# Expert tiles: half of each weight piece's subtractions a turn later, and one list multiply on another engine

## The reference, cut to what matters

```python
x = x + tanh(g_xattn) * attention(layernorm(x), ctx, ctx, fside, W1, b1, W2, b2)
h = layernorm(x).reshape(-1, 256)
route = softmax(h @ router_w + router_b, axis=1)
max_prob, max_ind = route.max(1, keepdims=True), argmax(route, 1)
for e in range(8):
    a, g = split(h @ w1[e], 2, axis=1)          # w1[e]: 256 x 2048
    y = silu(a) * g @ w2[e]                     # w2[e]: 1024 x 256
    out = where((max_ind == e)[:, None], y, out)
x = x + tanh(g_ffn) * out * max_prob
```

## Time and profile before

| | us |
|---|---|
| median of three runs | 448.81 |
| the profiled execution, its own time | 449.49 |
| its span, first to last instruction | 447.7 |
| TensorE (PE) busy | 401.3 |
| GpSimd (POOL) busy | 243.7 |
| VectorE (DVE) busy | 217.0 |
| ScalarE (ACT) busy | 176.5 |
| the 84 subtractions of L493, busy | 107.1 |
| TensorE's mean granted clock | 0.954 of full |

### The profile page before, as it was taken

How to read it: one execution, slowest core, us unless ns; L and a number is a source line. 1 busy time by engine, 2 the same in 40 slices (tenths; PEclk the granted TensorE clock), 3 DMA queues, 4 the chain that set the end, 5 groups by cost and what they waited for, 6 DMA issues and landing times.

```text
span 447.7 us, 9834 instructions
## 1 busy us (share of the span) xinstructions
PE 401.3 (90%) x2431; PEld 346.5 (77%) x2432; DVE 217.0 (48%) x527; ACT 176.5 (39%) x338; POOL 243.7 (54%) x324
## 2 busy tenths in 40 slices
PE   5998984149989999999999999999999999999990
PEld 4787872027878888888888888888888888888880
DVE  4689899933454443444433444433444434444340
ACT  1167650024443454545532344445433543233230
POOL 2356997221865577887772258728852676232221
PEclk9999897559999999999999999999999999999996
DMA  7950233863333044333442003433331011000010
GB/s 204 360 199 2 95 107 131 85 175 108 118 118 117 23 166 163 135 117 116 134 155 83 27 17 117 134 112 124 117 117 35 4 35 35 24 24 27 24 33 12
DMA packets 29850, 44.01 MB, mean 98 GB/s; under 512 B 8377, under 2 KB 25581, under 8 KB 27791
## 3 DMA queue, kind: packets, MB, share of 16 engines
q1 hardware_dynamic: 24095, 34.45, 24.6%
q0 software_dynamic: 3456, 9.11, 6.3%
q10 hardware_dynamic: 2288, 0.33, 0.5%
HBM read 35.44 MB, written 8.83 MB: 99 GB/s over the span
## 4 chain that ended last, share of the span: by engine, by line
PE 80%; DVE 7%; POOL 6%; DMA 2%; issue 2%; ACT 1%; DVEq 0%; SPq 0%; POOLq 0%; ACTq 0%
PE py L1117 22%; PE pa L1099 21%; PE pg L1099 21%; PE ph L1109 7%; POOL w_lo L415 2%; PE px L1084 2%; DVE x_all L742 1%; PE ps_s L1024 1%; POOL rstd L399 1%; DMA ctx_in<-in_ctx 1%; DVE bn L750 1%; DMA x_sorted<-residual_rows,idx_gather 1%; PE ps_p L968 1%; PE ps_xt L940 1%; DVE x_norm L878 1%
## 5 line engine op out<-in xcount | busy, mean ns | idle before, releaser
L895 DVE TENSOR_TENSOR ht_lo<-ph,ht_hi 128x512 fp32r<-128x512 f32 x70 | 48.4, 691 | 135.4 <-ACT ht_hi L624 135.4
L493 POOL TENSOR_TENSOR w_lo<-staging,w_hi x84 | 107.1, 1304 | 7.3 <-ACT w_hi L645 4.0
L624 ACT CAST ht_hi<-ph 128x512 fp32r<-128x512 f32 x70 | 41.1, 586 | 118.6 <-PE ph L1109 83.4
L1117 PE MATMUL py<-w_hi,ht_hi 128*128 x280 | 81.3, 291 | 0.8 <-DVE out_tile L903 0.8
L1117 PE MATMUL py<-w_lo,ht_hi 128*128 x280 | 78.4, 280 | 0.0
L1117 PE MATMUL py<-w_hi,ht_lo 128*128 x280 | 78.3, 280 | 0.0
L482 POOL DMA_INDIRECT out<-out_tile,idx_now x34 | 34.6, 1019 | 72.6 <-DVE out_tile L903 72.0
L1099 PE MATMUL pa<-w_hi,xt_hi 128*128 (+1 forms) x140 | 58.7, 420 | 0.8 <-ACT xt_hi L606 0.8
L443 POOL DMA_INDIRECT x_sorted<-residual_rows,idx_now x34 | 35.6, 1048 | 39.5 <-DVE x_norm L878 21.4
L1099 PE MATMUL pg<-w_lo,xt_hi 128*128 (+1 forms) x140 | 55.9, 400 | 0.0
L1099 PE MATMUL pg<-w_hi,xt_hi 128*128 (+1 forms) x140 | 55.9, 399 | 0.0
(11 more groups left out here) (168 smaller groups left out, 583.2 us busy)
## 6 DMA issues: line engine op xcount, KB each, us to landing
staging<-in_L_ffn_w SPq DMA_DIRECT2D x24, 1024.0 KB
residual_rows<-x_all SPq DMA_DIRECT2D x8, 516.0 KB, 4.0
x_all<-in_x SPq DMA_DIRECT2D x8, 512.0 KB, 10.1
x_sorted<-residual_rows,idx_now POOLq DMA_INDIRECT x34
out<-out_tile,idx_now POOLq DMA_INDIRECT x34, 2.5
w_in<-in_L_xattn_W SPq DMA_DIRECT2D x2, 256.0 KB, 4.7
ctx_in<-in_ctx SPq DMA_DIRECT2D x1, 308.0 KB
mask_in<-in_fside_1xSxS ACTq DMA_DIRECT2D x1, 308.0 KB, 11.7
```

The costliest lines, as they stand in the source:

```text
L493: lo = nc.gpsimd.tensor_tensor(out=w_lo[:, bass.ds(dst + q * QW, QW)], in0=staging[:, bass.ds(src + q * QW, QW)], in1=w_hi[:, bass.ds(dst ...
L624: nc.scalar.copy(ht_hi[:, j], ph[j][:]).then_inc(hhi_ready[j], 1)
L895: nc.vector.tensor_tensor(out=ht_lo[:, j], in0=ph[j][:], in1=ht_hi[:, j].bitcast(FP32), op=ALU.subtract).then_inc(hlo_ready[j], 1)
L1117: last = mm(py[:, 0:D], ht[:, j, c * P:(c + 1) * P], w[:, bass.ds(slot + (DC * PW + (j * HC + c) * D), D)], start=j == 0 and n == 0, stop= ...
```

## The change

The multiply of round 0 moves from GpSimd to VectorE, between the comparison of round 0 and those of round 1, and the semaphore `token_ready` goes. `low_part` is split into two halves of two subtractions. The first stays where it was, behind the store of the turn. The second comes in the following turn, between the gather and the store, and adds to `w_ready`. Each half reads the piece's number and branches for itself. A last second half stands behind the loop.

```diff
-            end_group = ROUNDS[0][1]
-            pool.wait_ge(col_ready, 1)
-            nc.gpsimd.tensor_tensor(out=col_hot[:, 0:end_group], in0=col_hot[:, 0:end_group],
-                                    in1=token_of[:, 0:end_group].unsqueeze(2).to_broadcast([P, end_group, COLS, B]),
-                                    op=ALU.mult).then_inc(token_ready, 1)
-
...
-            def low_part(t):
+            def low_half(t, half):
 
                 piece = pool.value_load(tile_piece[:, bass.ds(t, 1)], min_val=0, max_val=E * PIECES - 1)
                 with pool.If(piece > 0):
                     src = pool.snap((piece % PIECES) * PW)
                     dst = pool.snap(((piece // PIECES) & 1) * EW + src)
-                    pool.wait_ge(w_hi_ready, piece + (N_CHUNK - PIECES + 1))
-                    for q in range(QUARTERS):
+                    if half == 0:
+                        pool.wait_ge(w_hi_ready, piece + (N_CHUNK - PIECES + 1))
+                    for q in range(half * QUARTERS // 2, (half + 1) * QUARTERS // 2):
                         lo = nc.gpsimd.tensor_tensor(out=w_lo[:, bass.ds(dst + q * QW, QW)],
                                                      in0=staging[:, bass.ds(src + q * QW, QW)],
                                                      in1=w_hi[:, bass.ds(dst + q * QW, QW)].bitcast(FP32),
                                                      op=ALU.subtract)
-                    lo.then_inc(w_ready, 1)
-
+                    if half == 1:
+                        lo.then_inc(w_ready, 1)
 
             def tile(t):
                 index_copies(t)
                 pool.wait_ge(xnorm_ready, t + 2)
                 pool.wait_ge(res_ready, t + 2)
                 gather_rows(t + 2, idx_now[:, 0:1])
+                low_half(t - 1, 1)
                 scatter(t - 1, out_tile)
-                low_part(t)
-
-            low_part(0)
+                low_half(t, 0)
+
+            low_half(0, 0)
             tile(1)
             with pool.Fori(2, total) as t:
                 tile(t)
+            low_half(last_tile, 1)
...
-                slots = nc.vector.tensor_tensor(out=slot_hot[:, at], in0=of_group(slot_iota, P),
-                                                in1=of_token(pos_f[:, 1], P), op=ALU.is_equal)
-                if r == 0:
-                    slots.then_inc(hot_ready, 1)
-                else:
-                    dve.wait_ge(col_ready, r + 1)
-                    nc.vector.tensor_tensor(out=col_hot[:, at], in0=col_hot[:, at], in1=of_token(token_v[:], COLS),
-                                            op=ALU.mult).then_inc(hot_ready, 1)
+                nc.vector.tensor_tensor(out=slot_hot[:, at], in0=of_group(slot_iota, P), in1=of_token(pos_f[:, 1], P),
+                                        op=ALU.is_equal)
+                dve.wait_ge(col_ready, r + 1)
+                nc.vector.tensor_tensor(out=col_hot[:, at], in0=col_hot[:, at], in1=of_token(token_v[:], COLS),
+                                        op=ALU.mult).then_inc(hot_ready, 1)
...
-                if r == 0:
-                    pe.wait_ge(token_ready, 1)
                 pe.wait_ge(hot_ready, r + 1)
```

More of the change, by code:

```diff
@@ L275, in flamingo_block @@
         col_ready = sem("col_ready")
-        token_ready = sem("token_ready")
         hot_ready = sem("hot_ready")
```

## The result

| | before | after |
|---|---|---|
| median, us | 448.29 (447.25 to 449.14, 4 runs) | 456.4 (454.87 to 457.59, 4 runs) |
| the profiled execution, us | 449.49 | 456.28 |
| its span, us | 447.7 | 454.4 |
| stores, issue to landing, us, median / longest | 2.5 / 3.3 | 4.4 / 6.0 |

The ratio is 1.0159, 95% interval 1.0117 to 1.0201: the change makes the kernel 1.6% slower. I had forecast 448.2 us with a range up to 450.0. Two executions far above all others, 689.88 us of e3 and 1035.74 us of the kernel before, measured beside e10 and e11, are left out of what follows.

A forecast was written before the change was run, and what follows sets the result against it. TensorE was taken to bound the kernel, with 80% of the chain. The terms -0.67 - 1.57 + 1.56 = -0.68 us gave 448.8 from the profiled execution and 448.1 from the median; forecast 448.2 us, range 446.8 to 450.0.

The forecast's parts named there:

- What else moves: Other turns: staging reload some 2.2 us later with 9.5 us of cover, store waiting for `out_tile` anyway; no cost.
- The multiply: List building before the first gather: VectorE's list ends earlier and the gather follows it; -0.67 us.
- the gate stores: Possible next release for the first gather: longest landing 91.1, ahead of the list's 91.33, so taken as not binding.
- Turn 2: `x_norm` no longer held up by GpSimd's subtractions, so TensorE's wait before `px` goes; -1.57 us.
- My third rival: Turn 2's long wait is an accident of the profiled execution; gain there only 0.3 us, total 449.4 us; chance 0.13.
- The handover: After each of two three-tile experts, TensorE waits 0.78 us for piece 1's second half; +1.56 us, bounds 0.52 to 1.83 each.
- My first rival: Handovers after three-tile experts cost more, from 1.12 us each up to 1.83, giving 450.2 us; chance 0.14.
- my second one: Clock rises before tile 0's products, 446.6 us, or later, 449.7 us; chance 0.14, half each way.

The follow-up runs named there:

- e3: Changed kernel, with the store's index copied after the second half, so the gather no longer waits for the last store; 451.93 us, ratio 1.0069.
- e10: Changed kernel, with the reload of pieces 0 and 1 held until the first half behind the store is finished; 452.08 us, ratio 1.006.
- e11: As e6, with halves in turn 2 too (turns 0 to 2); 447.74 us, ratio to before 0.9966.
- e1: Kernel before with only the multiply of round 0 moved to VectorE, low_part left whole; 450.2 us, ratio 1.0041.
- e5: Changed kernel with halves in turns 0 and 1 alone, whole pieces subtracted in the loop from turn 3; 452.23 us, ratio 1.0077.
- e8: Kernel before, unchanged, profiled a second time; 449.73 us, one run.
- e9: Kernel before, with only SyncE's load of piece 4 held until the first gather has landed; 447.59 us, ratio 0.9984.
- e2: Kernel before with only the subtractions halved, the multiply left on GpSimd; 456.31 us, ratio 1.0179.
- e4: Changed kernel, with the staging reload let go by an added branch after the next turn's index copies; 453.13 us, ratio 1.0137.
- e7: Changed kernel, with the reload of pieces 0 and 1 held for a semaphore GpSimd raises on reaching the next first half; 460.35 us, ratio 1.0283.
- e6: As e5, with SyncE's load of piece 4 held until the first gather has landed; 447.47 us, ratio to before 0.9988.

## Why the prediction was wrong

The step that failed is "What else moves", which stood in the sum at nothing: it took the later reload and the later store for harmless. The reload now makes the store land 4.4 to 6.0 us after its issue, and with the clock behind it the two handovers cost 3.69 + 3.02 = 6.71 us where I had 1.56 and, as the upper bound, 3.66. A second term that I put at nothing without a reason is the first gather's landing, 2.2 us longer.

- **The multiply.** Stretch of 1.09 us gone, one multiply added: 0.68 us from the first comparison to the gather, where I had 0.67. That this reaches the end was wrong. I named the gate stores as the next release and they were not; what I missed is the gather's own landing, which I left at its old 4.0 us. The load of piece 4 was issued in e1, the changed kernel and e5 from 0.3 us before the gather to 0.2 after; `x_norm` began 5.2, 6.2 and 5.9 us behind it. Alone (e1) the edit costs 0.4% in place of a gain of 0.67 us.
- **Turn 2.** -1.57 us, right: the wait fell from 1.68 to 0.10. My third rival, that the long wait was an accident of one execution, is refuted by e8 and e9; e1 shows that it can still be shorter.
- **The handover.** Place and number were right, and the reason for a part of it; the size was not: idle times of 1.87 and 2.74 us for 0.78. My first rival had the direction and the place, but its bound of 1.83 us rested on the second branch's register work, and that was not what came. Of the 1.09 us that the first is over, TensorE's wake-up is about a quarter (0.34 us from the last subtraction's end, where I took 0.1 from a VectorE row); most of the rest is the copies' later start, 162.87 with the halves ended at 162.03. With the landing out of the way (e10, e3) the idle times are 1.04, 1.01, 1.25 and 1.18, near the forecast of 0.78 with the measured wake-up, about 1.0.
- **What else moves.** I wrote that the reload comes 2.2 us later, with 9.5 us of cover, and that the store waits for `out_tile` anyway. The first is true: no cast waited for a load. The second is nearly so: the store is issued 1.3 to 1.4 us after the start of `out_tile` as before, and up to 1.2 us later than that in eleven turns. Both looked only forward along their own line. I priced the load for the cast that needs it and not for the store that it now runs into, and the store for being late at its issue and not for being late at its landing, for which `index_copies` waits.
- **The clock.** That it would fall again behind such a wait stood in no rival; my second one spoke of tile 0 alone. It made 3.69 us of an idle time of 1.87. In the profiles of this study it fell behind one of the two handovers in the changed kernel, e2, e4 and e7 (idle times there of 1.87 to 3.43 us) and behind none in e3 and e10 (1.25 us at most). The length of the idle time does not tell by itself: it fell behind 1.93 us in e5 and not behind 1.94 in e6, nor behind the 2.74 and 2.80 of the second handover in the changed kernel and e2.

The account of the two profiles, from `out_tile` to `out_tile`, after less before: +1.02 for the first one, -1.57 in turn 2, +3.69 and +3.02 at the handovers, +0.53 in the turn of 240.4, where `x_norm` and TensorE wait 0.29 us; together 6.69, and 439.97 - 433.27 = 6.70. The +1.02 is made of -0.76 before the lists, -0.68 in the lists, +2.16 for the gather and +0.30 from `x_norm` to the first `out_tile`.

The stretch before the lists is touched by no edit, and yet the first comparison begins between 82.8 and 86.1 us in the 13 profiles. So the spans of two profiles can differ by 3 us for no reason of the edit, and the stretch from the lists on is the surer one to compare. What makes this difference is open. The medians differ by 8.1 us and the two profiled executions by 6.8, because the profiled one of before, at 449.49, lies above the four of the table.

## What to carry to other kernels

When a step moves on an engine whose semaphore lets a transfer go, ask for that transfer twice: when it is needed, and which small transfer it will now be issued just ahead of. A small store or gather that somebody waits for should be issued well clear of a megabyte's load, here 2.7 us or more behind it or 3.7 ahead of it; a hold on the load that costs no instruction (another semaphore for an instruction that is there) brought 4.3 of 8 us back. Read a wait on a landing as a link of the chain even where it has ended early so far.

## What the runs showed of the hardware

**A store against a load.** Where a staging load (1 MB, from SyncE) was issued 2.7 to 3.3 us ahead of a store (17 stores in each of the two profiles of the kernel before and in e9's), the store landed 2.4 to 3.4 us after its issue. Where the load was issued between 1.2 us ahead and 0.7 us behind the store's start (18 stores each in the changed kernel, e2 and e7), it took 4.4 to 6.0 us. With no load near, 2.2 to 2.5. Most of the delay comes before the store's own data moves. Counted from the issue, its first packet of 4096 bytes starts after 1.6 us where no load is near, after 3.1 to 4.3 us in the changed kernel with a load near, and after 3.2 to 4.9 in e7. Issue order alone does not tell: GpSimd's store is issued for 1.02 us, and the packets of a load that SyncE issued within this time started first. Why is open.

**Two engines at one port.** `x_norm` waits for GpSimd's subtractions, but not at every boundary of them. Behind four subtractions it got in when it began 2.30 to 2.34 us after the first (0.40 to 0.41 us long, in every such turn of seven profiles), and at 1.63 to 1.98, where it ended 2.7 us after the first, that is behind the second. At 2.35 (e5, e6) it waited to the end of the fourth, 2.81 us. At 3.22 it waited to the end of the fourth in three profiles (1.98 us) and only to the third in e1 (0.71 us). If 2.35 us is where it turns, which two cases alone suggest, the kernel before, at 2.30 to 2.33 in its turns, runs a few hundredths of a microsecond from a wait of 2.4 us. The Trainium skill, "SBUF — State Buffer", section "SBUF: two separate sides", has the loser blocked for the whole instruction that holds the port; the runs agree that `x_norm` waits for a subtraction under way, and show that the wait can be for several instructions. What decides at a boundary is open.
